# Second attention: scores a quarter of a cycle sooner in TensorE's order, transposes of the weights and what follows from them a fifth of a cycle later

## The reference

```python
def _topk_cross_attn(h, ctx, w_q, b_q, w_kv, b_kv, w_co, b_co):
    q = (h @ w_q + b_q).reshape(B, L, H, D)
    kv = (ctx @ w_kv + b_kv).reshape(B, Lc, 2, H, D)
    k, v = (kv[:, :, 0], kv[:, :, 1])
    scores = jnp.einsum('bqhd,bkhd->bhqk', q, k) / jnp.sqrt(jnp.float32(D))
    top_s, top_i = jax.lax.top_k(scores, TOPK)        # TOPK = 16
    attn = jax.nn.softmax(top_s, axis=-1)
    vg = jnp.take_along_axis(v_bh[:, :, None, :, :], top_i[..., None], axis=3)
    o = jnp.einsum('bhqk,bhqkd->bqhd', attn, vg).reshape(B, L, C)
    return o @ w_co + b_co

def _swiglu(h, w_m1, b_m1, w_m2, b_m2):
    u = h @ w_m1 + b_m1
    a, b = (u[..., :HID], u[..., HID:])
    return jax.nn.silu(a) * b @ w_m2 + b_m2
```

## Time and profile before

| | us |
|---|---|
| median of 3 runs | 1518.57 |
| lowest and highest run | 1518.34, 1521.01 |
| the profiled execution | 1521.19 |
| its span, first to last instruction | 1519.4 |
| the second attention in it | some 415 (195 to 610) |

### The profile page before, as it was taken

One profiled execution on the slowest core, in us unless ns is written; L12 is line 12 of the kernel. 1 busy time (PEld: TensorE's weight loads), 2 busy tenths in 40 slices (PEclk: granted clock), 3 DMA queues, 4 the chain that ended last, 5 costly groups with the idle time before them and its releaser, 6 DMA issues.

```text
span 1519.4 us, 25438 instructions
## 1 busy us (share of the span) xinstructions
PE 1379.1 (91%) x9100; PEld 691.2 (45%) x9100; DVE 918.1 (60%) x2815; ACT 713.3 (47%) x1454; POOL 342.0 (23%) x377
## 2 busy tenths in 40 slices
PE   7999887779889977999899999999999999988998
PEld 4467554444544544353233333333333335544675
DVE  3555487987787788675465666667676436650220
ACT  2255454647347345304644465555656674544221
POOL 1011167775555567000000000000000010010120
PEclk9899988879979988999999999999999999999999
DMA  5100002000000000000002000000000000000000
GB/s 189 50 22 26 20 18 99 22 2 1 1 15 2 1 28 1 27 1 1 1 2 69 2 1 2 1 2 1 2 12 1 2 2 2 13 3 3 14 18 28
DMA packets 22093, 26.74 MB, mean 18 GB/s; under 512 B 4205, under 2 KB 19635, under 8 KB 21709
## 3 DMA queue, kind: packets, MB, share of 16 engines
q1 hardware_dynamic: 21059, 25.03, 5.1%
q10 hardware_dynamic: 909, 0.10, 0.0%
HBM read 21.58 MB, written 3.08 MB: 16 GB/s over the span
## 4 chain that ended last, share of the span: by engine, by line
PE 66%; DVE 9%; issue 3%; ACT 3%; POOL 2%; DMA 1%; ACTq 0%; SPq 0%; POOLq 0%; DVEq 0%
PE bank L1076 24%; PE bank L1033 11%; PE bank L1116 8%; PE bank L1048 7%; PE bank L1012 3%; PE bank L991 3%; DVE x_hat L1495 2%; PE bank L1140 2%; PE bank L970 1%; PE bank L1159 1%; DVE left L1550 1%; PE bank L1018 1%; DVE left L1557 1%; DVE part_max L1522 1%; DVE top L1547 1%
## 5 line engine op out<-in xcount | busy, mean ns | idle before, releaser
L1306 ACT ACTIVATE pr<-bank 128x512 f32<-128x512 f32 x656 | 353.4, 598 | 289.4 <-PE bank L1076 276.2
L1522 DVE TENSOR_REDUCE part_max<-bank 128x1 f32<-128x512 f32 x512 | 327.0, 684 | 180.6 <-PE bank L1076 180.1
L1076 PE MATMUL bank<-slot 32*128 32x512 f32 (+1 forms) x3072 | 385.5, 521 | 10.4 <-ACT pr L1306 6.1
L1076 PEld LDWEIGHTS bank<-slot 32*128 32x128 f32 x3072 | 160.6, 186 | 210.3 <-issue 159.9
L1572 POOL TENSOR_SCALAR var_eps<-mean_var 128x4 f32<-128x4 f32 x24 | 5.6, 232 | 920.2 <-DVE mean_var L1486 920.2
L1628 POOL TENSOR_SCALAR left<-left 128x308 f32<-128x308 f32 x128 | 125.3, 979 | 105.2 <-ACT exp_all L1328 50.8
L1116 PE MATMUL bank<-pr,v 128*17 128x512 f32 x1024 | 135.3, 600 | 0.2
L1033 PE MATMUL bank<-h_t,w_m 128*128 128x512 f32 x256 | 130.7, 637 | 4.4 <-DVE o_all L1466 3.2
L1630 POOL TENSOR_TENSOR probs<-left,exp_all 128x308 f32<-128x308 f32 x128 | 107.4, 839 | 10.7
L1547 DVE MAX8 top<-bank 128x8 f32<-128x154 f32 x256 | 69.4, 312 | 50.0 <-PE bank L1140 39.0
L1328 ACT ACTIVATE exp_all<-bank,neg 128x154 f32<-128x154 f32 x256 | 85.7, 387 | 11.2 <-DVE left L1550 6.8
(11 more groups left out here) (140 smaller groups left out, 1775.6 us busy)
## 6 DMA issues: line engine op xcount, KB each, us to landing
w_m<-in_L_xcond_w_m SPq DMA_DIRECT2D x1, 2048.0 KB, 8.4
w_m<-in_L_xcond_w_m SPq DMA_DIRECT2D x2, 1024.0 KB, 8.1
w<-in_L_xcond_w SPq DMA_DIRECT2D x2, 1024.0 KB, 6.4
w_ada<-in_L_xcond_w_ada SPq DMA_DIRECT2D x1, 1792.0 KB, 10.6
x_sb<-in_x SPq DMA_DIRECT2D x6, 256.0 KB, 6.6
res_row<-rows_dram SPq DMA_DIRECT2D x12, 128.0 KB, 3.4
out_x<-x_sb SPq DMA_DIRECT2D x6, 256.0 KB, 2.1
wa<-in_L_xcond_w_qkv SPq DMA_DIRECT2D x1, 768.0 KB, 7.0
```

What stands on the lines that cost most here:

```text
L1076: last = nc.tensor.matmul(g.bank(*tile)[:, into], left, right, start=True, stop=True)
L1306: nc.scalar.activation(m.pr[:, u % NPR, :], g.bank("s", gi, i)[:, :], ACT.Exp).then_inc(g.free("s", gi, i), 1)
L1522: nc.vector.tensor_reduce(m.part_max[:, slot, h * TB + i // 8, i // 4 % 2:i // 4 % 2 + 1], bank[:, :], axis=AX.X, op=ALU.max).then_inc(don ...
```

## The change

It moves due times in `topk_run` and nothing else. The scores are due 1.05 instead of 0.8 cycles ahead of their cycle, the transposes 2.1 instead of 1.9 behind its start, and their copy, the products with the values and the three steps behind these are each 0.2 of a cycle later as well. No instruction, buffer, bank number, semaphore or DMA is added or taken away by hand.

```diff
@@ -470,20 +470,20 @@
                 for t in range(4 * half, 4 * half + 4):
                     t0 = start + u * step
-                    plan.at(t0 - 0.8 * step, ("c_score", gi, t, 0), ("c_score", gi, t, 1), ("c_scores", gi, t))
+                    plan.at(t0 - 1.05 * step, ("c_score", gi, t, 0), ("c_score", gi, t, 1), ("c_scores", gi, t))
                     for hf in range(2):
                         t1 = t0 + 0.5 * hf * step
                         plan.at(t1, ("c_top", gi, t, hf))
                         plan.at(t1 + 0.12 * step, ("c_neg", gi, t, hf))
                         plan.at(t1 + 0.25 * step, ("c_exp_all", gi, t, hf))
                         plan.at(t1 + 0.55 * step, ("c_pick", gi, t, hf))
-                    plan.at(t0 + 1.9 * step, ("c_tail", gi, t), ("c_turn", gi, t))
-                    plan.at(t0 + 2.0 * step, ("c_copy", gi, t))
+                    plan.at(t0 + 2.1 * step, ("c_tail", gi, t), ("c_turn", gi, t))
+                    plan.at(t0 + 2.2 * step, ("c_copy", gi, t))
                     if t % 4 == 3:
-                        plan.at(t0 + 2.3 * step, ("c_pv", gi, half))
-                        plan.at(t0 + 2.75 * step, ("o_copy", gi, half))
-                        plan.at(t0 + 3.1 * step, ("o_turn", gi, half))
-                        plan.at(t0 + 3.6 * step, ("o_norm", gi, half))
+                        plan.at(t0 + 2.5 * step, ("c_pv", gi, half))
+                        plan.at(t0 + 2.95 * step, ("o_copy", gi, half))
+                        plan.at(t0 + 3.3 * step, ("o_turn", gi, half))
+                        plan.at(t0 + 3.8 * step, ("o_norm", gi, half))
```

## The result

| | kernel before | changed kernel |
|---|---|---|
| median | 1519.45 us | 1539.86 us |
| lowest and highest | 1518.34, 1521.01 | 1533.85, 1539.90 |
| ratio to the kernel before, 95% interval | | 1.0117 [1.0099, 1.0135] |
| the profiled execution (its span) | 1521.19 (1519.4) | 1539.90 (1538.1) |

The change costs 1.2%, about 20 us. The forecast was 1531 with a range of 1514 to 1541: the sign is right, and the time lies 9 us above the forecast, 1 us inside the upper end of the range.

A forecast was written before the change was run, and what follows sets the result against it. DVE was taken to bound 197 to 302 and PE the two MLP runs, with norm chains between. Terms 10.4 + 5 + 3 - 2 - 4 = +12.4 us gave 1531 against the median 1518.57, range 1514 to 1541.

The forecast's parts named there:

- the new waits behind `silu`: Four `silu` runs in the MLP runs: scores keep only F2 as cover, waits 14.4 less 4.0, +10.4 us.
- the clock and `down`: Behind the new `silu` waits: lower PE clock, +5 us, from 0 to 10; the 3.08 wait ahead of `down` stays.
- the small waits: Two-piece projection read-outs, transposes after an o_copy, ring banks changing hands: +3 us, from 0 to 5.
- the norm chains: Behind the `down` slots: DVE comes sooner into the norm and the low clock shortens, -4 us, from -7 to 0.
- the stretch bound by DVE: From 197 to 302: sooner scores find DVE busy anyway, one place at POOL's gating pays, -2 us, from -4 to 0.
- ACT becomes a loop: Rival for ordinary cycles: the chain closes within one cycle; 0.3 us short in 64 cycles, 19 us more, 1550; chance 0.05.
- Third stretch: nothing: From 531: held by the second gating of `w_m`, whose load waits for the last `down`, so no change.

The follow-up runs named there:

- late `silu`: `silu` due 0.65 instead of 0.25 of a step behind its slot: 1525.92 us against the changed kernel, 1519.09 us against the kernel before.

## Why the prediction was right, and where it was wrong

**Right: the new waits behind `silu`.** The step said that with F2 alone as cover they are 2.1, 4.3, 3.7 and 4.3 us, 14.4 in all. In the changed kernel they are 2.50, 4.54, 3.60 and 4.54, 15.2 in all; less the 4.0 of the earlier trace rows that is +11.2, forecast +10.4. Timeline of PE and ACT at the second run, as in the earlier trace rows:

```profile
364.50 3.60 PE L1033 MATMUL bank<-h_t,w_m 128*128 128x512 f32 x8
372.64 1.40 PE L1140 MATMUL bank<-kc,slot 32*128 32x154 f32 x8 [4.54 <-ACT exp_all L1328]
...
367.13 1.28 ACT L1289 ACT_TABLE_LOAD   x1
368.42 2.00 ACT L1289 ACTIVATE hidden<-hidden 128x1024 f32<-128x1024 f32 x2
...
370.54 1.28 ACT L1328 ACT_TABLE_LOAD   x1
371.83 0.67 ACT L1328 ACTIVATE exp_all<-bank,neg 128x154 f32<-128x154 f32 x2
```

Between the end of F2 at 368.10 and the scores at 372.64 PE has nothing that it may do. By an estimate from the drain that the Trainium skill, ScalarE: Activation LUTs, section What ACT_TABLE_LOAD costs, counts for each switch, each run with its two switches would have been 2.76 us longer; the next instruction starts 0.01 behind the load here too, and the waits came out as the rows alone gave them.

**Right: the clock and `down`; the small waits in their sum.** The clock cost +6.3 us in the two MLP runs (the PE busy column), forecast 5. The rest of the idle time there is 14.1 - 11.2 = 2.9, forecast 3, but that is partly luck. Scores behind a projection that is read out in two pieces did wait 0.71 us, forecast 0.6, but at cycles 42 and 58, outside these runs. Inside them the scores of two ordinary cycles waited 0.40 each, the transposes behind an o_copy 0.3 and not 1.0, and most of the rest came from places that were not named: 0.8 us of line 1033 for `hid`, and 0.7 more of line 1172 for the copied transposes. The scores at 372.64 took 1.40 us where those of the earlier trace rows took 0.79: they ran at the low level behind a wait in which PE did nothing. The wait ahead of `down` stayed: 2.92 us. And late `silu` shows that cover is what was lost at these four places: with it, sooner scores alone cost nothing. The whole change keeps 6.8 us of its loss even so (1525.92 against 1519.09), so in it the order costs something of its own.

**Nearly right: the norm chains.** Between the runs the kernel gained 2.5 us, forecast 4, within the bounds of 0 to 7. The wait ahead of on_turn, 1.88 in the earlier trace rows, is 0.30. But PE idled for 1.4 us more there, with new waits of scores, 1.72 the longest; the gain is the 3.8 us of busy time at a clock of 0.86 instead of 0.80.

**Wrong: the stretch bound by DVE.** The step read that sooner scores find DVE busy anyway, and set -2 with bounds of -4 to 0. Measured: +7.4, 9 us off, the largest error of the sum. The gain itself came: the maxima won 2.4 us from cycle 8 to cycle 16, and with the new due times below 18 alone cycles 0 to 22 took 2.7 us less. But the step looked only at who is late now. It didn't close the chain for the new order with the slot in it: that takes 5.12 us at the full clock and 6.69 at 0.74, while the scores of the kernel before followed one another there every 4.37. Not all of the +7.4 is this loop: the kernel with the new due times from 18 on loses 2.0 us in the same stretch, at cycles 21 and 22. The rival "ACT becomes a loop" had the right mechanism, was given 0.05, and was priced at the wrong place, in the MLP cycles. There its 0.2 us to spare held: scores waited in two ordinary cycles alone, 0.40 us each.

**Missed: the stall behind the stage.** "Third stretch: nothing" left out that the late o_norm of the last cycles changes the order of the banks beyond the stage. That gave 3.6 us back. Without it the time would have left the range: that it lies inside is luck, one error of the sum against another.

The sum was 12.4 and came to 18.7: 9.4 us too low in the first stretch, 2.0 in the MLP runs and 1.5 in the norms, against 1.0, 3.6, 0.4 and 1.6 that came back from the end of the stage on and ahead of it.

**Open.** Why the clock stays up in one execution and falls in another isn't shown. In cycle 16, with the same list up to there, it fell in the changed kernel: 1.00 from 277.00 to 283.80, then 0.67 to 304.30. In the profile with the new due times below 18 it was 1.00 from 278 to 304. The two groups of that first kernel hint at both cases, but its profile shows one side only, and ten times with a gap of 3.1 us can be scatter. The 1.0 us that came back at the end of the stage, 3.6 of busy time less 2.6 of new idle time, was not taken apart.

## What to carry to other kernels

When a step is moved sooner in an in-order queue, write down what stands between it and the step that its buffers wait for, for every kind of cycle: the ordinary one hid its chain by 0.2 us, four with a table switch lost 11. Then close the loop once with the durations at full clock and once at the low one; an order that just fits at the full clock need not fit below it. And before giving up a move, see what else is in the chain: here the table switch could be moved out of it, and the same sooner scores came out 0.5% faster instead of 0.6% slower, 0.25% of it from the late `silu` alone.

## What the runs showed that was not expected

- The same work can repeat to 0.01 us: the kernel with the last cycles moved has the two MLP runs at 77.16 and 75.73 us, as the kernel before, though it entered the stage 3.0 us sooner. But it need not: with the new due times below 18 alone, which leave the MLP runs as they were, the first took 78.27 us, with PE idle for the same 5.27 and the clock at 0.96 instead of 0.98. So compare the clock of a stretch before its length is put down to an edit.
- The clock can be part of a loop: the same piece of the list took 6.69 us at 0.74 and 5.12 at 1.00. In the first MLP run the changed kernel took 87.15 and, in its repeat, 87.10 us, but with the old order ahead of it 83.26, with PE idle for 11.1 us instead of 11.4: 3.6 us come from the clock alone.
